# Attention's weighted sum in groups of two key tiles every two steps, in place of groups of four every four steps

## What is computed

```python
x = x + _L0_conv_ref(_gn(x), L0_conv_weight)
t = _to_tokens(x)                     # (8, 3136, 64)
t = t + _L1_attn_ref(_ln_t(t), ...)   # softmax(q k^T / 8) v, over the 3136 tokens of an image
t = t + _L1_ffn_ref(_ln_t(t), ...)    # top 2 of 16 experts, silu(h1) * h2, then w3
x = _from_tokens(t, x)
```

## Time and profile before

| what | value |
|---|---|
| median of 3 runs | 2943.6 us |
| the profiled execution: its own time, its span | 2947.36 us, 2945.6 us |
| TensorE busy | 2612.0 us, 89% |
| VectorE busy | 1928.1 us, 65% |
| ScalarE busy | 1300.6 us, 44% |
| GpSimd busy | 1020.2 us, 35% |
| chain that ended last, by engine | PE 57%, DVE 17%, issue 7%, POOL 2% |
| granted clock of TensorE, mean | 0.958 |

### The profile page before, as it was taken

One profiled execution on the slowest core, in us unless ns is written; L12 is line 12 of the kernel. 1 busy time (PEld: TensorE's weight loads), 2 busy tenths in 40 slices (PEclk: granted clock), 3 DMA queues, 4 the chain that ended last, 5 costly groups with the idle time before them and its releaser, 6 DMA issues.

```text
span 2945.6 us, 47190 instructions
## 1 busy us (share of the span) xinstructions
PE 2612.0 (89%) x14013; PEld 1663.2 (56%) x14013; DVE 1928.1 (65%) x5389; ACT 1300.6 (44%) x2985; POOL 1020.2 (35%) x1093
## 2 busy tenths in 40 slices
PE   4899989999999999999999999999999999987772
PEld 2455555565656566565656656565655656554661
DVE  4577676766676676767776676767776766763432
ACT  1344444454444444454444545454444545443441
POOL 2022014200343045412452136321552136445656
PEclk8899999999999999999999999999999999997775
DMA  2133101111211122111212122111211112112332
GB/s 61 32 84 75 37 25 43 42 38 29 61 51 47 39 57 59 50 50 37 70 48 53 41 53 65 53 47 39 62 50 48 34 39 62 43 50 68 96 92 48
DMA packets 226462, 153.00 MB, mean 52 GB/s; under 512 B 100144, under 2 KB 216624, under 8 KB 226224
## 3 DMA queue, kind: packets, MB, share of 16 engines
q1 hardware_dynamic: 192112, 98.97, 12.7%
q0 software_dynamic: 31456, 48.03, 6.9%
q10 hardware_dynamic: 2656, 2.98, 0.4%
HBM read 83.92 MB, written 65.27 MB: 51 GB/s over the span
## 4 chain that ended last, share of the span: by engine, by line
PE 57%; DVE 17%; issue 7%; POOL 2%; ACT 1%; DMA 1%; SPq 1%; ACTq 0%; POOLq 0%; DVEq 0%
PE ps_o L1378 14%; PE ps_m L1341 8%; PE ps_s L1364 7%; DVE max_part L1041 5%; PE ps_s L1366 5%; PE ps_x L1522 5%; PE ps_z L1537 3%; PE ps_z L1404 3%; PE ps_z L1507 2%; PE ps_s L1522 2%; POOL got L728 2%; PE ps_y L1457 1%; PE ps_x L1530 1%; PE ps_y L1441 1%; DVE up L1196 1%
## 5 line engine op out<-in xcount | busy, mean ns | idle before, releaser
L1041 DVE TENSOR_REDUCE max_part<-ps_m 112x1 f32<-112x448 f32 x1568 | 950.7, 620 | 624.7 <-PE ps_m L1341 607.5
L886 ACT ACTIVATE prob<-ps_s 128x448 f32<-128x448 f32 x1400 | 751.7, 541 | 889.5 <-PE ps_s L1366 874.6
L1341 PE MATMUL ps_m<-k_a,q_a 128*112 128x448 f32 (+2 forms) x1792 | 611.3, 372 | 70.6 <-DVE max_part L1041 56.6
L1378 PE MATMUL ps_o<-prob,v_s 128*64 128x448 f32 x2800 | 629.6, 558 | 0.0
L1364 PE MATMUL ps_s<-q_a,k_a 128*128 128x448 f32 x1400 | 590.0, 421 | 18.6 <-issue 12.7
L707 POOL DMA_INDIRECT sorted_x<-xn,slot x448 | 433.0, 967 | 244.6 <-issue 197.5
L1366 PE MATMUL ps_s<-q_b,k_a 128*128 128x448 f32 x1400 | 512.1, 366 | 0.0
L728 POOL DMA_INDIRECT got<-sorted_y,slot x448 | 427.3, 954 | 186.4 <-issue 123.0
L746 POOL TENSOR_TENSOR ln_s<-ln_s,minus_half 112x4 f32<-112x4 f32 x56 | 57.9, 1035 | 1246.8 <-DVE ln_s L951 1086.0
L1341 PEld LDWEIGHTS ps_m<-k_a,q_a 128*112 128x112 f32 x1792 | 305.0, 177 | 280.4 <-DVE max_part L1041 162.5
L1364 PEld LDWEIGHTS ps_s<-q_a,k_a 128*128 128x128 f32 x1400 | 264.9, 189 | 208.1 <-issue 178.8
(11 more groups left out here) (184 smaller groups left out, 2944.1 us busy)
## 6 DMA issues: line engine op xcount, KB each, us to landing
fx<-sorted_x SPq DMA_DIRECT2D x43, 384.0 KB
sorted_y<-fy SPq DMA_DIRECT2D x49, 320.0 KB, 3.0
fx<-sorted_x SPq DMA_DIRECT2D x50, 256.0 KB
xh<-in_x SPq DMA_DIRECT2D x96, 126.0 KB, 2.7
sorted_x<-fy POOLq DMA_DIRECT2D x28, 320.0 KB, 6.0
sorted_x<-xn,slot POOLq DMA_INDIRECT x448
got<-sorted_y,slot POOLq DMA_INDIRECT x448
x_now<-in_x SPq DMA_DIRECT2D x112, 56.0 KB, 2.3
```

The lines of the kernel that those rows point to most:

```text
L886: a.activation(prob[(at.n * KEY_TILES + i) % PROBS][:], ps_s[(at.n * KEY_TILES + i) % 2][:, 0:CHUNK], ACT.Exp).then_inc(s["p_ready"], 1)
L1041: v.tensor_reduce(max_part[:, m % PER, m // PER:m // PER + 1], ps_m[m % 2][0:TILE, 0:CHUNK], AX.X, ALU.max).then_inc(s["max_red"], 1)
L1341: done = t.matmul(ps_m[m % 2][0:TILE, first:last], q_a[:, bass.ds(n % QUERIES, 1), j * TILE:(j + 1) * TILE].rearrange("p a c -> p (a c)"), ...
L1378: t.matmul(ps_o[side:side + CHANNELS, 0:CHUNK], v_s[u % 2][:, i, :], prob[(n * KEY_TILES + i) % PROBS][:], start=(i < 2), stop=(i >= KEY_T ...
```

## The change

The step's condition and the number of tiles a call weighs are changed. `weigh` runs in every odd step from 5 to 23, on tiles 0 and 1, then 2 and 3, up to 18 and 19. The last group of five stays in step 1 of the next chunk, and `GROUP`, which sets `first` and `LAST_GROUP`, stays 4.

```diff
-            def weigh(n, u, first):
+            def weigh(n, u, first, many=2):
...
-                for i in range(first, KEY_TILES if first == LAST_GROUP else first + GROUP):
+                for i in range(first, KEY_TILES if first == LAST_GROUP else first + many):
                     pe.wait_ge(s["p_ready"], ONE + n * KEY_TILES + (i + 1))
                     side = 64 * (i % 2)
                     t.matmul(ps_o[side:side + CHANNELS, 0:CHUNK], v_s[u % 2][:, i, :], prob[(n * KEY_TILES + i) % PROBS][:],
...
                     first = i - 1 - GROUP
-                    if i % GROUP == 1 and first >= 0 and at.attends:
+                    if i % 2 == 1 and 0 <= first < LAST_GROUP and at.attends:
                         weigh(at.n, at.u, first)
```

## The result

| what | before | after |
|---|---|---|
| median of 4 runs each | 2944.4 us (2940.9 to 2949.07) | 2914.23 us (2912.85 to 2919.01) |
| the profiled execution: its own time, its span | 2947.36, 2945.6 us | 2912.85, 2910.9 us |
| granted clock, mean | 0.958 | 0.959 |

The ratio is 0.9899 with an interval of 0.9881 to 0.9917: **1.0% faster**, 30.2 us between the medians. The forecast was 2924, 20 us. Between the two profiled executions it is 34.5 us (34.7 between their spans), and what follows divides those.

What follows compares the result with a forecast made beforehand. TensorE was taken to bound the kernel, 94% busy over chunks 11 to 55. 61 us added, 67 and 14 given back make -20 against the profiled 2947.4: 2927, less 3.8 to the median, 2924 us; range 2878 to 2978.

Steps and rivals of the forecast that it cites:

- three stalls: TensorE waits for VectorE's chains in steps 16, 20 and 23 of chunk 33: 0.51, 0.93 and 0.53 us, all should go.
- The rival that the ends decide: Slower: group ends cost more than the stalls removed; 2996 us, or 2965 with the discounts standing; chance 0.25.
- the one that the two cancel: Cost and gain cancel: time stays within 0.2%, which is 5.9 us; chance 0.13.
- the one that all stalls go: All stalls go and VectorE has room in every kind of chunk: -64 us, 2880 us; chance 0.15.
- The price of the ends: Extra groups: 0.24 us each in steps 7, 15, 23, 0.33 in 19, none in 11; 61 us added over all chunks.
- What is given back: Stalls removed in chunks 11 to 55: 1.5 us a chunk, 67 us; lower bound half, upper 103 us.
- The kept part of the stalls: Of 1.97 us a chunk, 1.57 kept, after taking off 0.3 for step 16 and 0.1 for step 20.
- Kind 0: Chunks of kinds 0 and 3: routing keeps VectorE busy in steps 14 to 22, so a moved pair covers nothing new.
- Kinds 1, 2 and 5: Chunks of these kinds become some 0.5 us shorter, kind 6 most, kind 3 the same.
- First 11 chunks: Chunks without experts: 14 us added by group ends, 14 us given back from two waits.
- elsewhere nothing moves: Outside the counted ends and stalls: no exponential late, no instruction or semaphore added, the order of steps stays.
- Signs: Profile after: x4 blocks about 0.91 us, waits of lines 1422 and 1530 almost gone, 1341 halved, VectorE's idle pieces smaller.

Runs made afterwards that it cites:

- late: Kernel before with the change's pairs in steps 15, 19 and 23 only, groups of four kept in 5 and 9: 2907.03 us, ratio 0.988.
- split: Kernel before with the groups of four in steps 5 and 9 cut in two by the step's own maximum, no work moved to another step: 2980.6 us, ratio 1.0116.
- early: Kernel before with the change's pairs in steps 7 and 11 only, groups of four kept in 13, 17 and 21: 2950.26 us, ratio 1.0026.
- lastconv: Kernel before with step 1's last group of five moved behind the second maximum, right ahead of the convolution: 3267.16 us against 3259.76, ratio 1.0029.
- move19: Kernel before with step 17's group cut in two, its second pair moved to step 19; on a chip with 3264.13 us before: ratio 0.9981.

## Why the prediction was right, and where its sizes were off

- **Direction and mechanism: right.** The new pairs stand in front of three stalls and take their place. *late* has this half alone and gains more than the change. The rival that the ends decide (2965 to 2996) fell, the one that the two cancel (within 0.2%) too; the one that all stalls go (2880) fell as well, with 30 us of waits (21.2 + 4.8 + 3.9) left of the 82.6 that I had added up from the earlier trace rows.
- **The price of the ends was too low.** I put 0.24 on steps 7, 15 and 23, since the scores behind transposes already pay the way out. They do pay it, and the group pays more all the same: 0.30 in steps 7 and 15. With 0.33 for step 19, where the price held (+0.33), and nothing in step 11, where it held too (the gate's start moved by the pair's 0.75 alone), a chunk costs 1.23 and not 1.05 (step 23 taken as 7 and 15), 45 chunks 55 and not 47 us. *split* has 0.32 for the full 0.33.
- **What is given back was too low**, and by more: the mis-sized term. "I take the ordinary chunk less a little, 1.5 x 45 = 67 us": the ledger has -27.0 over 44 chunks, with 44 x 1.23 = 54 paid, so about 81 us came back, 1.84 a chunk. 1.3 us of them are the clock in chunk 13, a term the prediction doesn't have. Two larger parts of it:
  - The kept part of the stalls. I took off 0.3 for `down` and `hidden` of step 16, which take less time behind a stall; it is 0.16 (1.15 against 0.99). In kind 1 the three stalls gave 0.32, 0.75 and 0.65, together 1.72.
  - Kind 0. I said that there and in kind 3 a moved pair covers nothing new. For kind 3 the mean is -0.10 a chunk, and that is luck: the five chunks go from -1.14 to +1.01, with falls of the clock in step 21 or 22 of some, and by steps there are both gains (16: -0.83, 13: -0.54, 21: -0.49) and losses (15: +0.60, 10: +0.45, 23: +0.22). Kind 0 lost 0.75 us a chunk. By the ledger (its pairs' 0.75 taken out) step 7 is -0.26, which step 10 gives back (+0.27), step 15 is -0.68 and step 19 -0.16: its stalls stand in other steps, and the pairs cover these. *early* has the first two alone, *late* the others. I had read the ordinary chunk and reasoned about the other kinds from the routing, without reading a chunk of kind 0.
- **Kinds 1, 2 and 5** were forecast at some -0.5: -0.49, -0.59, -0.77. "Kind 6 most": -1.14. Right.
- **First 11 chunks.** 14 us paid and 14 back were forecast, nothing in sum; it is -7.2. The two waits of the earlier trace rows gave 13.2 us by their modelled ends as expected, and the ends cost less than forecast (+0.25 each in steps 7 and 15). Of the 7.2 us, 1.4 are the clock in chunk 6. Not foreseen was the gate's wait in step 10 (5.8 to 11.8 us), which took over most of step 9's: "elsewhere nothing moves" was wrong there.
- **Signs.** x4 blocks of 0.90 (forecast 0.91); line 1530 gone; line 1422 from 15.9 to 4.8, not all; line 1341 from 39.6 to 21.2, about half; VectorE's idle time in smaller pieces. A block of four records with transposes behind costs 1.05, under my limit of 1.3.
- **The sum.** Forecast 61 - 67 - 14 = -20. Of the trace: about 54 and 12 paid, 81 and 19 back, -34, and -30 in the medians. Both sides were too small, the cost by 5 us and the gain by 19, and the one error hid some of the other.

## What to carry to other kernels

A block of work with no urgent result of its own (here a weighted sum that may come four steps late) is a cover: its place should be between the start of another engine's chain and the point at which this engine meets its end. Move it there first, and cut it into smaller blocks only as far as places need it, for each cut has a price at its ends, here 0.3 us of an engine that is 94% full. Five pairs more a chunk gained 1.0%; the same places with one group more gained 2.2%.

## What the runs showed of the hardware that was not expected

- The price of going from 128 or 112 columns to 64 and back, alone: 0.32 us in the kernel's time and 0.34 in its steps (*split*). It goes with the columns, not with the stage: the convolution with 64 columns joins a group of 64 without a gap (*lastconv*), while the gate's fp32 matmuls with 112 columns, behind a group in step 11, start 0.90 behind the group's first, as the 448-column scores do:

```profile
1601.22 0.97 PE L1378 MATMUL ps_o<-prob,v_s 128*64 128x448 f32 x4
1602.12 0.96 PE L1457 MATMUL ps_y<-gate_s,xn2T 128*112 128x16 f32 x8
```

- Other 64-column work can start beside a lone tile: two records of the convolution start at 265.88 and soon after, ahead of the tile's second record at 266.25. That they use the half that the tile leaves free is my reading; the trace doesn't name the half.
- The clock fell behind some waits of TensorE and not behind others of the same length. In chunk 6 the kernel before waits 1.37 us in step 16 and has a granted clock of 0.60 in step 17; *move19* waits 1.36 us in the same place and has 1.00 behind it, and *lastconv* has 1.00 around its wait of 1.35 us in chunk 15. What decides it is not shown. A change of the order can thus win or lose 1.4 us in a place where it removes no wait.
- The same kernel took 2944 us on one chip and 3260 and 3264 on two others, with mean granted clocks of 0.958 and about 0.914. On these two, engines stop for some us with nothing to wait for that the trace shows, mostly in steps 14 to 21 (31 of the 39 steps of *lastconv* that are over 2 us longer), never in the first image. Of ScalarE, in *lastconv*:

```profile
1506.44 0.54 ACT L887 ACTIVATE prob<-ps_s 128x448 f32<-128x448 f32 x1 [7.93 <-issue]
```

  And of the waits of VectorE in the same kernel, where "remote" is a releaser that the trace doesn't name:

```profile
DVE max_part L1042 <- remote: 148.9, 58, 9.2
```

  The kernel before has no such wait on the chip with 2944 us. What causes it stays open, the chip or something beside the kernel. An effect of 0.1% can't be told there from the total, but can be from the steps that the pauses spare.
